# Value projection of a cross-attention kernel: each 512-column matmul issued as two of 256 columns in the same PSUM bank

## The reference

```
xn  = layernorm(x over channels and positions) * gamma + beta
q   = Wq xn + bq ;  k, v = Wkv ctx + bkv        (8 heads of 64 channels each)
att = softmax(q^T k / sqrt(64))                 (256 queries x 256 keys per head)
out = x + Wo (att v, heads side by side) + bo
```

## Time and profile before

| | us |
|---|---|
| median of 3 runs | 257.28 |
| lowest and highest run | 256.77, 259.45 |
| span of the profiled execution, first to last instruction | 255.2 |
| own time of the profiled execution beside its span | not shown |

### The profile page before, as it was taken

One profiled execution on the slowest core, in us unless ns is written; L12 is line 12 of the kernel. 1 busy time (PEld: TensorE's weight loads), 2 busy tenths in 40 slices (PEclk: granted clock), 3 DMA queues, 4 the chain that ended last, 5 costly groups with the idle time before them and its releaser, 6 DMA issues.

```text
span 255.2 us, 8140 instructions
## 1 busy us (share of the span) xinstructions
PE 229.4 (90%) x2746; PEld 203.3 (80%) x2746; DVE 211.6 (83%) x446; ACT 203.2 (80%) x391; POOL 198.5 (78%) x188
## 2 busy tenths in 40 slices
PE   0571969999999999999999999999999999999982
PEld 0571747888898889888888898888888889888871
DVE  2399998899988888888888888888888888887875
ACT  2343345999899999999999999999999989998970
POOL 3047968577999797979797979797979888989580
PEclk9999996899999999999999999999999999999997
DMA  6999402010111111112121212121212121010000
GB/s 141 215 293 213 98 0 84 25 52 14 53 44 55 44 55 38 56 31 62 32 62 32 62 32 62 32 62 32 62 32 62 33 64 35 13 32 13 13 4 22
DMA packets 13412, 15.08 MB, mean 59 GB/s; under 512 B 2064, under 2 KB 11920, under 8 KB 13200
## 3 DMA queue, kind: packets, MB, share of 16 engines
q1 hardware_dynamic: 13072, 14.16, 20.9%
q10 hardware_dynamic: 320, 0.66, 1.2%
HBM read 5.90 MB, written 1.05 MB: 27 GB/s over the span
## 4 chain that ended last, share of the span: by engine, by line
PE 71%; DVE 17%; DMA 4%; issue 3%; ACT 2%; POOL 2%; SPq 0%; POOLq 0%
PE ps_sc L380 12%; PE ps_max L399 11%; PE ps_sc L381 10%; PE ps_t L362 7%; PE ps_z L416 6%; PE ps_z L418 5%; PE ps_m L451 5%; PE ps_z L417 5%; PE ps_t L363 5%; DMA x_res<-x_tiles 4%; DVE neg_max L733 4%; PE ps_m L450 4%; DVE t_b L717 3%; DVE x_all L644 2%; DVE x_seq L644 1%
## 5 line engine op out<-in xcount | busy, mean ns | idle before, releaser
L605 POOL TENSOR_TENSOR p_lo<-p_full,p_hi 128x512 f16<-128x512 f32 x122 | 144.9, 1194 | 32.6 <-ACT p_full L525 31.2
L733 DVE TENSOR_REDUCE neg_max<-ps_max 128x2 f32<-128x512 f32 x128 | 84.5, 664 | 0.0
L523 ACT ACTIVATE p_hi<-ps_sc 128x512 f16<-128x512 f32 x128 | 76.1, 595 | 5.0 <-PE ps_sc L381 0.6
L525 ACT ACTIVATE p_full<-ps_sc 128x512 f32<-128x512 f32 x128 | 76.6, 599 | 0.6 <-POOL p_lo L605 0.6
L380 PE MATMUL ps_sc<-t_a,c_seq 128*128 128x256 f32 x256 | 73.0, 306 | 0.0
L381 PE MATMUL ps_sc<-t_b,c_seq 65*128 65x256 f32 x256 | 67.6, 284 | 0.0
L416 PE MATMUL ps_z<-u_hi,p_hi 128*128 128x65 f16 x512 | 60.8, 196 | 1.2 <-POOL p_lo L605 1.0
L417 PE MATMUL ps_z<-u_lo,p_hi 128*128 128x64 f16 x512 | 59.6, 193 | 0.0
L418 PE MATMUL ps_z<-u_hi,p_lo 128*128 128x65 f16 x512 | 59.3, 193 | 0.0
L416 PEld LDWEIGHTS ps_z<-u_hi,p_hi 128*128 128x128 f16 x512 | 45.6, 97 | 7.3 <-DVE z_n L740 0.7
L380 PEld LDWEIGHTS ps_sc<-t_a,c_seq 128*128 128x128 f32 x256 | 49.3, 193 | 0.7 <-issue 0.6
(11 more groups left out here) (100 smaller groups left out, 310.6 us busy)
## 6 DMA issues: line engine op xcount, KB each, us to landing
ctx_raw<-ctx SPq DMA_DIRECT2D x8, 256.0 KB, 16.4
c_seq<-c_all SPq DMA_DIRECT2D x16, 128.0 KB, 2.0
x_seq<-x_all SPq DMA_DIRECT2D x14, 128.0 KB, 2.0
c_max<-c_all SPq DMA_DIRECT2D x14, 128.0 KB, 2.0
x_res<-x_tiles SPq DMA_DIRECT2D x4, 256.0 KB, 7.1
z_n<-ctx_flat SPq DMA_DIRECT2D x1, 1024.0 KB, 13.6
c_seq<-c_all SPq DMA_DIRECT2D x16, 64.0 KB, 2.0
out<-x_res SPq DMA_DIRECT2D x16, 64.0 KB, 1.7
```

Source lines behind the costliest of these rows:

```text
L523: nc.scalar.activation(p_hi[:, buf, :, :].rearrange("p t s -> p (t s)"), scores, ACT.Exp).then_inc(act_phi, 1)
L525: nc.scalar.activation(p_full[:, head % 2, :], scores, ACT.Exp).then_inc(act_p, 1)
L605: nc.gpsimd.tensor_tensor(p_lo[:, buf, :, :].rearrange("p t s -> p (t s)"), p_full[:, head % 2, :], p_hi[:, buf, :, :].rearrange("p t s -> ...
L733: nc.vector.tensor_reduce(neg_max[:, (par + dn) % 2, head, :], ps_max[:, head % 2, :].rearrange("p (t s) -> p t s", t=KT), X, ALU.max, neg ...
```

## The change

The two 512-column matmuls of a projection step become four of 256 columns: first both terms for columns 0 to 255 (heads 0 to 3), then both terms for columns 256 to 511. Weights and operands are the same; each weight tile is loaded twice. The semaphore is raised by the last of the four.

```
-                    mm(ps_m[:], c_seq[:, q, 0, keys], b_w[:, 0, :], start=True, stop=False)
-                    mm(ps_m[:], c_seq[0:C, q, 1, keys], b_w[0:C, 1, :], start=False, stop=True).then_inc(pe_u, 1)
+                    for half_heads in range(2):
+                        cols = slice(half_heads * S, (half_heads + 1) * S)
+                        mm(ps_m[:, cols], c_seq[:, q, 0, keys], b_w[:, 0, cols], start=True, stop=False)
+                        last = mm(ps_m[:, cols], c_seq[0:C, q, 1, keys], b_w[0:C, 1, cols], start=False, stop=True)
+                    last.then_inc(pe_u, 1)
```

## The result

| | before | after |
|---|---|---|
| median of 4 runs, us | 257.74 (256.77 to 259.45) | 268.5 (267.22 to 274.19) |
| ratio | | 1.0373, 95% interval 1.0293 to 1.0453 |
| span of the profiled execution, us | 255.2 | 272.4 |

The change makes the kernel 3.7% slower.

What follows compares the result with a forecast made beforehand. PE was taken as the bound: 30 steps at 0.41 us plus early 0.6 and 0.5 gave 13.4 us, less a 0.5 us wait, 12.9; span 268.1 plus 2.1 made 270.2 us, 8-in-10 range 263.5 to 273.

Steps and rivals of the forecast that it cites:

- What the loads wait for: Projection matmuls: going from 128 contracted rows to 64 or fewer, and back, exposes the next load, about 0.20 us each.
- The price per step: Each projection step: four alternations at 0.31 us, 1.24 us against 0.83 us, so plus 0.41 us.
- The steady part: From 62.5 us on, 28 steps on a saturated PE, each plus 0.41 us; one 0.5 us DVE wait absorbs part.
- The early steps: Four projections at 40.82, 45.76, 49.20 and 56.02 us: plus 0.6, about 0.5, 0.41 and 0.41 us.
- the one at 49.20: Third early projection, at 49.20 us: full clock and saturated PE, so counted at the full 0.41 us.
- The step at 56.02: Fourth early projection, at 56.02 us: full clock and saturated PE, so counted at the full 0.41 us.
- The last step: Projection at 237.6 us, where ACT is nearly the bound: PE's delay still shows, counted in full at 0.41 us.
- The sum: All steps together: 13.4 us, less PE's 0.5 us wait for DVE, so 12.9 us added to the span.
- Width: Rival: 512-column matmuls keep the next load waiting, so splitting saves 0.38 us per step, 245.7 us; chance 0.12.
- Half price: Rival: bubble only where 512 columns drain, exposed load at every alternation; plus 0.22 us per step, 264.0 us; chance 0.08.
- Neutral: Rival: the exposure belongs to the step, not each matmul; 0.83 us stays, 257 to 258 us; chance 0.05.

Runs made afterwards that it cites:

- experiment 2: Kernel before, still 512 columns, but the second projection matmul contracts 65 rows instead of 64, the added row zero: 246.52 us, ratio 0.954.
- experiment 4: Kernel before with only the 64-row projection matmul halved into two of 256 columns, three matmuls per step: 258.91 us, ratio 1.0004.
- Experiment 7: Kernel before with the second matmul of the scores at 64 rows instead of 65, omitting the row that subtracts the maximum: 477.38 us in one run.
- experiment 1: The changed kernel run again without any edit: 270.92 us median, ratio 1.036 against the kernel before.
- experiment 11: Kernel before with the split into 256 columns only in the later 28 projection steps, the first four whole: 269.47 us, ratio 1.0417.
- experiment 10: Kernel before with the split into 256 columns only in the four projection steps of the first two sequences: 258.86 us, ratio 1.0016.
- experiment 6: Changed kernel with four pairs of 128 columns instead of two of 256, eight row-count changes per step: 296.54 us, ratio 1.1544.
- experiment 5: Changed kernel with both 128-row matmuls first, then both 64-row ones, each overwriting its columns: 258.24 us, ratio 1.0064 against the kernel before.
- 9 with 32 rows: Kernel before with 32 instead of 64 rows in the second projection term, at 512 columns: 255.2 us in one run.

## Why the prediction was right, and which terms were off

**What the loads wait for: right.** The weak point of the argument was that width and row count changed together, with one tiny 1-row matmul to decide. Experiments 2 and 4 settle it: 65 for 64 rows at 512 columns removes the wait, and 256-column matmuls of 64 rows next to each other do not have it. Experiment 7 is the converse at 256 columns. The Trainium skill says that changing the tiling mode drains the TensorE (TensorEngine Tiling (Array Packing), Key Properties). The runs agree as far as a change of row count costs time, 0.20 us; that the hardware changes a mode between 64 and 65 rows is still an inference from the times, since no row names one. For matmuls one behind the other the Trainium skill (TensorE: Matmul & The Clock Gate, Back-to-back issue gap) gives columns / 2.4 + 2.5 ns, 0.109 us for 256 columns and 0.216 for 512. Where no row count changes the spacings here come near it and stay somewhat above: 0.117 to 0.12 us at 256 columns, 0.24 at 512 (experiment 2).

**The price per step: right.** Forecast plus 0.41 us, measured 1.23 - 0.83 = 0.40 us, and 1.58 - 1.18 = 0.40 us up to the second L362.

**The steady part: right.** From the fifth projection to the last there are 27 intervals, and 27 x 0.41 less the 0.5 that a DVE wait absorbs was 10.6 us. The two ends, in the kernel before 62.52 us and 237.56 us, here as rows of the changed kernel (experiment 1):

```profile
67.79 0.36 PE L452 MATMUL ps_m<-b_w,c_seq 128*128 128x256 f32 x1
...
253.09 0.36 PE L452 MATMUL ps_m<-b_w,c_seq 128*128 128x256 f32 x1
```

185.30 us against 175.04, plus 10.3; the first profile after gives 185.31. The absorbed part is seen too: PE's wait for L717's `t_b` is gone in the profile after, and the interval from the fifth to the sixth projection is 7.30 us in experiment 1 against 7.29 before.

**The early steps: the terms hold at the lower clock only.** They were to give 0.6 + 0.5 + 0.41 + 0.41 = 1.9 us. Where the lower clock lasts past the second projection they give 2.1 us (experiments 1 and 11): the chain of waits is on PE through the first three projections there. Where the clock rises soon they give 0.55 us in the profile of experiment 10 and 0.4 us by the ratio of its runs (0.16%, interval minus 0.3 to plus 0.6%). There the chain leaves PE after the first projection, at 44.98 us, for ACT and then for DVE. So the first two steps and the one at 49.20 were priced as if PE were the bound whatever the clock does, and "on a saturated PE" does not hold for the one at 49.20: its interval grew by 0.14 us, from 6.83 to 6.97, not by 0.41.

**The step at 56.02: right, against appearances.** In the kernel before, the chain from 50.98 to 66.98 us goes through DVE with no pause above 0.03 us, and that looks as if 0.40 us of PE could be hidden there. But the interval behind this step grew from 6.50 to 6.90 us, in full, and the next stayed at 7.30. The two projections in experiment 10:

```profile
57.56 0.36 PE L453 MATMUL ps_m<-b_w,c_seq 128*128 128x256 f32 x1
...
64.46 0.48 PE L453 MATMUL ps_m<-b_w,c_seq 128*128 128x512 f32 x1
```

The way from PE to DVE leads through POOL, in rows of the kernel before and then of experiment 10 (whose lines are numbered four higher):

```profile
59.28 2.33 POOL L605 TENSOR_TENSOR p_lo<-p_full,p_hi 128x512 f16<-128x512 f32 x2 [1.33 <-ACT p_full L525]
60.95 1.21 DVE L644 TENSOR_TENSOR x_all<-xn,x_all 64x512 fp32r<-64x512 f32 x1
```

```profile
61.22 2.33 POOL L609 TENSOR_TENSOR p_lo<-p_full,p_hi 128x512 f16<-128x512 f32 x2 [1.69 <-ACT p_full L529]
62.52 1.58 DVE L648 TENSOR_TENSOR x_all<-xn,x_all 64x512 fp32r<-64x512 f32 x1
```

`x_all` ends 0.55 us after POOL's `p_lo` in both (60.95 + 1.21 against 59.28 + 2.33, and 62.52 + 1.58 against 61.22 + 2.33). I infer that its duration holds a wait that no row names: 1.21 us in the one, 1.58 in the other, where the shortest of this line takes 0.69. POOL waits for ACT's exponential, and ACT waited for this step's last matmul, 0.27 us before and 0.67 in experiment 10. A chain without pauses on an engine is thus no proof that the engine sets the pace.

**The last step: mis-sized.** It was counted at its full 0.41 us. The next exponential (L526) does start 2.01 us after the projection instead of 1.70 (253.09 to 255.10, against 237.56 to 239.26 in the earlier trace rows), but from that projection to the end of the span it is 17.71 us in experiment 1 and 17.83 in experiment 11, against 17.64 before: 0.1 to 0.2 us are left. (The first profile after has 18.21 us, with a granted clock of 0.54 from 266 to 270 us, against 0.79 from 249 to 253 us before.) Where the drain of the pipeline gives the rest back is not shown; its chain goes over ACT, POOL and DVE.

**The sum.** 10.3 for the steady part, about 0.5 for the early steps at a clock that rises soon, and 0.1 to 0.2 for the last: about 11 us against the forecast 12.9. The medians of the first comparison differ by 10.8; the ratio 1.0373 is 9.6 us, with an interval of 7.6 to 11.7, so 12.9 is too much. The forecast of 270.2 us is only 1.7 above the measured 268.5, because the kernel before ran 0.5 us longer beside it (257.74) than in the median that I started from.

**The rivals.** Width (245.7 us) named by accident nearly the time of experiment 2, but by another mechanism: what the split would have bought, 65 rows buy without it. Half price is refuted by the bubble: every change costs 0.20 us at 128, 256 and 512 columns alike (experiment 6). Neutral is refuted by experiments 1 and 11.

**The better version.** Experiment 2 beats both kernels: two matmuls as before, one row more. Its steps save 1.18 - 0.79 = 0.39 us each, and ACT is at 145.01 of 152.50 us there (62.5 to 215 us), 95%. That little is left to win on PE alone is an inference from this share; no run tests it.

## What to carry to other kernels

Where fp32 matmuls that contract more than 64 rows alternate with ones of 64 or fewer (tested here: 128 and 65 against 64 and 32), look at the start of the weight loads: a load that starts with its own matmul costs about 0.2 us here, per change and whatever the width. Pad the short operand with a zero row beyond 64, or put the short ones side by side; splitting columns between them multiplies the changes. And before a stretch counts as bound by a busy engine, read the chain of waits of that same stretch, and hold start-to-start intervals of two runs at a like clock against each other: the chain can name an engine whose instruction is itself waiting.

## What the hardware showed that I had not expected

- A single row decides: 64 rows cost 0.20 us at each change, 65 cost none, 32 and 64 cost the same, and so do 65 and 128.
- DVE's L644 takes 0.69 us at its shortest, but the one that follows the fourth projection takes 1.08 to 1.59 us in seven profiles (before, experiments 1, 2, 5, 9 with 32 rows, 10 and 11) and ends 0.54 to 0.55 us after POOL's `p_lo` each time. What holds it is not shown.
- In experiment 7 TensorE was busy 240.00 of 240.00 us by the profile and was still granted only the 1.2 GHz level until about 330 us; the same kernel, with the same pattern of four changes of row count per head, had the full clock from 380 to 400 us. What the clock answered to is not shown.
- In the profile of experiment 1 the granted clock is recorded as 1.00 from 43 to 50 us, while matmuls of 256 columns start 0.21 us apart as at 1.2 GHz. The same holds in experiment 11 up to 51 us. There the spacings are to be believed:

```profile
45.16 0.41 PE L380 MATMUL ps_sc<-t_a,c_seq 128*128 128x256 f32 x1
45.38 0.41 PE L381 MATMUL ps_sc<-t_b,c_seq 65*128 65x256 f32 x1
45.59 0.41 PE L380 MATMUL ps_sc<-t_a,c_seq 128*128 128x256 f32 x1
```
